# A graph network of four layers on one core: edge arrays loaded in 112 and 13 rows, a fourth result buffer on a 320-float pitch, and the turns of C handed over in two halves

## The reference, cut to what matters

```
L0: h = relu(((1 + eps) h + sum of h[src] over edges into dst) @ W1.T + b1) @ W2.T + b2, then layernorm
L1: attention over the edges in 8 heads, @ Wo, layernorm, relu(@ W1 + b1) @ W2 + b2, layernorm
L2: edge weights exp(w - max w) / row sum; messages h @ Wm + bm both ways; @ W1, layernorm, relu, @ W2, relu
L3: relu(mean of h[src] over edges into dst @ W_l + b_l + h @ W_r)
```

## Time and profile before

| what | value |
|---|---|
| median of three runs | 1148.22 us (1144.56 to 1149.89) |
| profiled execution, its own time | 1147.85 us |
| its span in the trace | 1145.9 us |
| granted clock of the matmul engine, mean | 0.982 |
| instructions | 16827 |

### The profile page before, as it was taken

The page is one execution under the profiler, slowest core; times in us unless marked ns, Lnnn a source line. Parts: engine busy times, 40 slices in busy tenths (PEclk is TensorE's granted clock), DMA queues, the critical chain, the costliest instruction groups (busy, mean ns, idle before and its releaser), DMA issues.

```text
span 1145.9 us, 16827 instructions
## 1 busy us (share of the span) xinstructions
PE 1059.4 (92%) x5904; PEld 690.6 (60%) x5904; DVE 598.9 (52%) x1743; ACT 446.6 (39%) x762; POOL 157.9 (14%) x182
## 2 busy tenths in 40 slices
PE   5988978899999999899999999999899997999998
PEld 3455656655544555677777777774447895555443
DVE  6889999910685010565666656655456235400122
ACT  5601455510545101655656556552436424510000
POOL 0000000000044000333333100005546011000000
PEclk9999888899999999999999999999999998999999
DMA  5002588870010010545454200026001060100010
GB/s 167 1 0 84 160 267 270 266 243 1 1 62 1 1 37 1 183 137 152 141 154 121 89 1 1 2 83 241 1 1 46 1 224 1 37 1 1 9 46 35
DMA packets 73041, 93.63 MB, mean 82 GB/s; under 512 B 7113, under 2 KB 63120, under 8 KB 72966
## 3 DMA queue, kind: packets, MB, share of 16 engines
q1 hardware_dynamic: 72966, 92.62, 25.9%
HBM read 58.00 MB, written 34.60 MB: 81 GB/s over the span
## 4 chain that ended last, share of the span: by engine, by line
PE 78%; DVE 10%; issue 5%; ACT 3%; SPq 1%; DMA 1%; DVEq 0%; ACTq 0%
PE PS L557 8%; PE PS L788 8%; PE PS L771 7%; PE PS L590 7%; PE PS L929 7%; PE PS L743 7%; PE PS L964 6%; PE PS L714 5%; PE PS L613 5%; DVE HT L1099 2%; PE PS L529 2%; DVE R L1234 2%; PE PS L700 2%; PE PS L891 2%; PE PS L911 2%
## 5 line engine op out<-in xcount | busy, mean ns | idle before, releaser
L557 PE MATMUL PS<-HT,R 125*128 125x313 bf16 x636 | 140.2, 360 | 26.5 <-DVE HT L1099 14.9
L1223 DVE CUSTOM_DVE_ANT_0 HT<-PS,CD 128x1250 f32<-128x1250 f32 (+1 forms) x80 | 116.4, 1455 | 66.9 <-issue 66.9
L557 PEld LDWEIGHTS PS<-HT,R 125*128 x636 | 99.9, 172 | 67.3 <-issue 45.3
L771 PE MATMUL PS<-K,HT 128*128 128x128 f32 (+2 forms) x800 | 111.7, 278 | 15.8 <-DVE R L1234 15.0
L1528 ACT COPY R<-PS 128x512 f32<-128x512 f32 (+1 forms) x120 | 64.8, 575 | 120.1 <-PE PS L771 118.2
L1548 ACT ACTIVATE HT<-HT,soft 128x1250 f32<-128x1250 f32 (+1 forms) x80 | 107.2, 1340 | 10.4 <-DVE soft L1226 3.1
L771 PEld LDWEIGHTS PS<-K,HT 128*128 128x128 f32 (+2 forms) x800 | 83.4, 140 | 43.5 <-DVE R L1234 24.2
L1117 DVE TENSOR_SCALAR HT<-BC,HT 125x314 bf16<-125x314 f16 x316 | 92.1, 365 | 13.5 <-PE PS L557 10.8
L743 PE MATMUL PS<-R 64*128 64x512 f32 (+3 forms) x480 | 94.8, 527 | 3.1 <-DVE soft L1223 3.1
L788 PE MATMUL PS<-R 128*64 128x128 f32 (+2 forms) x1600 | 94.2, 273 | 0.0
L1438 ACT COPY X<-PS 128x626 f32<-128x626 f32 x80 | 52.5, 690 | 98.4 <-PE PS L557 97.5
(11 more groups left out here) (220 smaller groups left out, 1387.3 us busy)
## 6 DMA issues: line engine op xcount, KB each, us to landing
edge_parts<-X SPq DMA_DIRECT2D x160, 156.5 KB, 2.8
R<-edge_parts SPq DMA_DIRECT2D x60, 156.5 KB, 2.4
CD<-edge_sums SPq DMA_DIRECT2D x1, 6250.0 KB, 20.4
CD<-edge_parts SPq DMA_DIRECT2D x10, 469.5 KB, 3.9
BC<-edge_parts SPq DMA_DIRECT2D x30, 156.5 KB, 2.4
CD<-edge_parts SPq DMA_DIRECT2D x3, 1565.0 KB, 10.8
edge_sums<-R SPq DMA_DIRECT2D x20, 156.5 KB, 3.0
R<-edge_parts SPq DMA_DIRECT2D x18, 155.5 KB, 2.4
```

The lines of the kernel that those rows point to most:

```text
L557: return mm(bank(b0 + h, QUART), stat, hot, start=first, stop=True, skip_group_check=True)
L771: m = nc.tensor.transpose(PS[0:rows(j), o:o + n], Pb[u % 2][a][0:n, j * P:j * P + rows(j)], ident[0:n, 0:n])
L1223: ve.tensor_tensor_reduce(Pb[s][a][0:n], PS[0:n, a * N:(a + 1) * N], cd[0:n, t, :], 1.0, -3e38, ALU.add, ALU.max, soft[0:n, s, a:a + 1]).t ...
```

## The change

1. The three edge arrays are loaded in two DMAs each, rows 0 to 111 (`EVEN` = 112) and rows 112 to 124.
2. Tiles 3 to 9 of x at the start count on a semaphore of their own, `x_in2`, so ACT waits for these two DMAs and not for the seven behind them.
3. `winbuf` gets a fourth buffer, and its quarters stand on a pitch of 320 floats instead of 313 (`PITCH`; the array in DRAM had this pitch already). Four buffers of 1280 floats fill X to the end, so `self_cols` moves to WA. With that, all tiles of x can be reloaded at once behind the edge stage, and the V weights, which overwrite WA, are loaded behind `eps`.
4. A turn of C has two hand-overs: the first four transposes wait for ACT's copy of the turn before and release ACT's copy; the other six wait for DVE's copy and release DVE's.
5. `rows_in` and `out_done` become one semaphore, `rows_io`.

```diff
-WB_N = 3
+WB_N = 4
...
-        self_cols = X[:, :, :].rearrange("p t o -> p (t o)")[:, 3840:3840 + N]
-        winbuf = [X[:, :, :].rearrange("p t o -> p (t o)")[:, q * GH * QUART:(q + 1) * GH * QUART] for q in range(WB_N)]
+        self_cols = WA[:, 0:N]
+        winbuf = [X[:, :, :].rearrange("p t o -> p (t o)")[:, q * GH * PITCH:(q + 1) * GH * PITCH] for q in range(WB_N)]
...
-            return ("x_in0", 16) if t < 2 else ("x_in1", 32) if t < 3 else ("x_in", 9 * 16)
+            return ("x_in0", 16) if t < 2 else ("x_in1", 32) if t < 3 else ("x_in2", 32)
...
-            sp.dma_start(dstI, A["dst_cols"]).then_inc(sem("edges_in"), 16)
-            sp.dma_start(srcI, A["src_cols"]).then_inc(sem("edges_in"), 16)
-            sp.dma_start(ew, A["weight_cols"]).then_inc(sem("edges_in"), 16)
+            for tile, name in ((dstI, "dst_cols"), (srcI, "src_cols"), (ew, "weight_cols")):
+                for r0, r1 in ((0, EVEN), (EVEN, EC)):
+                    sp.dma_start(tile[r0:r1], A[name][r0:r1, :]).then_inc(sem("edges_in"), 16)
...
                     sp.dma_start(dram_p.rearrange("k q d n -> (k q) d n")[:, d0:d0 + SUB, :],
-                                 b[:, h * QUART:(h + 1) * QUART]).then_inc(moved, 16)
+                                 b[:, h * PITCH:h * PITCH + QUART]).then_inc(moved, 16)
...
-            load_x(0, 7, "x_in")
+            load_x(0, T - 1, "x_in")
+            load_last_x("x_in")
             sp.wait_ge(sem("hw"), T)
             sp.wait_ge(sem("l0_w_in"), 32)
+            sp.wait_ge(sem("eps"), 2 * T)
             for p in range(PAIRS):
...
-            sp.wait_ge(sem("eps"), 2 * T)
-            load_x(7, T - 1, "x_in")
-            load_last_x()
...
-                if j > 0:
-                    pe.wait_ge(sem("cs_ev"), j)
-                    pe.wait_ge(sem("cs_ev_dve"), j)
-                turn_sources(j, 3, "cs_ps")
+                m = rows(j)
+                for t in range(T):
+                    n = rows(t)
+                    if j > 0 and t == 0:
+                        pe.wait_ge(sem("cs_ev"), j)
+                    if j > 0 and t == BANK // P:
+                        pe.wait_ge(sem("cs_ev_dve"), j)
+                    i = nc.tensor.transpose(PS[0:m, 3 * BANK + t * P:3 * BANK + t * P + n], cd[0:n, t, j * P:j * P + m],
+                                            ident[0:n, 0:n])
+                    if t in (BANK // P - 1, T - 1):
+                        i.then_inc(sem("cs_ps"), 1)
...
-                dve.wait_ge(sem("cs_ps"), j + 1)
+                dve.wait_ge(sem("cs_ps"), 2 * j + 2)
...
-                act.wait_ge(sem("cs_ps"), j + 1)
+                act.wait_ge(sem("cs_ps"), 2 * j + 1)
```

More of the change, by code:

```diff
@@ L32 @@
 EC, NC = 125, 320
+EVEN = 112
 FIX = 2
@@ L309, in load_x, with load_last_x @@
                 sp.dma_start(X[:, t0:t1, :], A["x"][t0 * P:t1 * P, :].rearrange("(t p) f -> p t f", p=P)).then_inc(sem(name), 16)
[L311 to L315, removed]
-            sp.dma_start(dstI, A["dst_cols"]).then_inc(sem("edges_in"), 16)
-            sp.dma_start(srcI, A["src_cols"]).then_inc(sem("edges_in"), 16)
-            sp.dma_start(ew, A["weight_cols"]).then_inc(sem("edges_in"), 16)
+            def load_last_x(name):
+                sp.dma_start(X[0:rows(T - 1), T - 1, :], A["x"][(T - 1) * P:N, :]).then_inc(sem(name), 16)
+            sp.dma_start(growI, A["dst_rows"]).then_inc(sem("rows_io"), 16)
+            sp.dma_start(K1[:, :], A["k1"][:, 0:NK1]).then_inc(sem("rows_io"), 16)
+            for tile, name in ((dstI, "dst_cols"), (srcI, "src_cols"), (ew, "weight_cols")):
+                for r0, r1 in ((0, EVEN), (EVEN, EC)):
+                    sp.dma_start(tile[r0:r1], A[name][r0:r1, :]).then_inc(sem("edges_in"), 16)
             load_x(0, 2, "x_in0")
@@ L322, in _ @@
             sp.dma_start(K2, A["k2"]).then_inc(sem("x_in1"), 16)
-            load_x(3, T - 1, "x_in")
-            load_last_x()
+            load_x(3, T - 1, "x_in2")
+            load_last_x("x_in2")
             sp.dma_start(iota, A["iota"]).then_inc(sem("x_in"), 16)
@@ L335, in move_window @@
                 g, half = divmod(w, GH // 2)
-                b = winbuf[g % WB_N][:, half * 2 * QUART:(half + 1) * 2 * QUART]
+                b = winbuf[g % WB_N][:, half * 2 * PITCH:(half + 1) * 2 * PITCH]
                 moved = sem("win_moved%d" % (g % WB_N))
@@ L446, in _ @@
                 sp.wait_ge(sem("out_ready"), t + 1)
-                sp.dma_start(out[t * P:t * P + rows(t), :], X[0:rows(t), t, :]).then_inc(sem("out_done"), 16)
-            sp.wait_ge(sem("out_done"), 16 * T)
+                sp.dma_start(out[t * P:t * P + rows(t), :], X[0:rows(t), t, :]).then_inc(sem("rows_io"), 16)
+            sp.wait_ge(sem("rows_io"), 2 * 16 + 16 * T)
         @block.tensor
@@ L983, in _ @@
             ve.memset(x_sq[:, :], 0.0).then_inc(sem("x_stats_free"), 1)
-            dve.wait_ge(sem("rows_in"), 2 * 16)
+            dve.wait_ge(sem("rows_io"), 2 * 16)
             link(ve.tensor_copy(growF, growI))
@@ L990, in _ @@
             i.then_inc(sem("setup_dve"), 1)
-            dve.wait_ge(sem("edges_in"), 3 * 16)
+            dve.wait_ge(sem("edges_in"), 6 * 16)
             ve.tensor_reduce(wmx[:, 0:1], ew, AX.X, ALU.max).then_inc(sem("setup_dve"), 1)
@@ L1068, in _ @@
             dve.wait_ge(sem("setup_ps"), 8)
-            dve.wait_ge(sem("x_in"), 9 * 16)
+            dve.wait_ge(sem("x_in"), 7 * 16)
             for q in range(FIX):
@@ L1437, in _ @@
                 o = (build_bank(2 * w // GH) + 2 * (w % 2)) * BANK
-                sc.copy(winbuf[g % WB_N][:, half * 2 * QUART:(half + 1) * 2 * QUART].rearrange("p (h n) -> p h n", h=2),
+                sc.copy(winbuf[g % WB_N][:, half * 2 * PITCH:(half + 1) * 2 * PITCH].rearrange("p (h n) -> p h n", h=2)[:, :, 0:QUART],
                         PS[:, o:o + 2 * BANK].rearrange("p (h n) -> p h n", h=2)[:, :, 0:QUART])\
@@ L1644, in _ @@
             pool.wait_ge(sem("bc_in"), 48)
-            pool.wait_ge(sem("x_in"), 9 * 16 + 48)
+            pool.wait_ge(sem("x_in"), 7 * 16 + 32)
             shift_and_add("l0", bc0[:, 2, :], ybuf)
```

## The result

The changed kernel takes 1141.99 us (median of 14 runs, 1138.69 to 1146.03) beside 1150.04 us for the kernel before (14 runs): ratio 0.9925, 95% interval 0.9907 to 0.9942, or 8.6 us less. The profiled execution took 1138.75 us, a span of 1136.7 us, against 1147.85 us and 1145.9 us.

What follows compares the result with a forecast made beforehand. PE, busy 92% of the span, was taken as the bound, so only its waits and late start counted. 1147.85 - 3.8 (start) - 5.4 (turns and clock) = 1138.65 us, as a median 1139.0 us; range 1134.5 to 1145.0 us.

Steps and rivals of the forecast that it cites:

- landmarks that the prediction named for the start: Start: DVE's first reduction near 6.5 us, ACT's first tile 8, PE 13, tile 3 18.5, first edge product 56.5.
- split, its three issues paid: Start: edge arrays spread over more DMA engines bring x 3.3 to 3.6 us earlier; three extra issues cost 0.3 us.
- own semaphore: Start: ACT's wait for tile 3 no longer includes the bias columns, 0.8 us earlier.
- both, first edge product: Start: split and own semaphore together, -3.8 us, carried through to the edge stage; ends -4.5 and +0.6.
- buffers and pitch: Edge stage: fourth buffer and wider pitch give 0, ends -0.9 and +0.5 us; at most ACT's 0.9 us wait goes.
- second hand-over: Turns of C: first four transposes run under DVE's copy, 1.5 us in turns 1 to 3 and 1.5 us later.
- clock in the turns: Turns of C: shorter PE waits keep the clock up, worth 2.4 us beyond the hand-over's 3.0 us.
- x had all but finished about 0.8 us before the bias columns: Start: step that sized the semaphore's gain at 0.8 us, from packet sizes between 20 and 22 us.
- the split spreads nothing: Rival at the start: the split does not free the DMA queue, start gives -0.5 to +0.6 us, 1144.0 us; chance 0.12.
- the 1 us that I had named as a sign against me: Edge stage: a length differing from 168 us by more than 1 us would show the prediction wrong.
- The cover: V products: weights issued later would still land 15.1 us before the first V product, so the term is 0.
- The case that the clock stays up: Turns of C: clock does not fall, turns give -5.4 us, chance 0.42; the rival that it falls, 1141.4 us, 0.30.

Runs made afterwards that it cites:

- e1: Also e1_split: only the split of the edge arrays into 112 and 13 rows, against the kernel before; ratio 0.9980.
- e4: Also e4_xin2: only the own semaphore for tiles 3 to 9 of x, against the kernel before; ratio 1.0007.
- e8: Also e8_nobuf: the whole change without fourth buffer, pitch of 320 floats and the loads these move; ratio 0.9934 against the kernel before.
- e3: Also e3_buffers: only the fourth buffer, pitch of 320 floats and moved loads of x and V weights, against the kernel before; ratio 0.9985.
- b0: The kernel before with the edit all experiments carry, edge-stage inner loops starting at a maximum, no value changed; ratio 1.0006.
- e5_half: The whole change with edge arrays cut into 62 and 63 rows instead of 112 and 13; ratio 0.9968 against the kernel before.
- e2_turns: Only the two hand-overs in the turns of C, against the kernel before; ratio 0.9929.
- e7_pad: The whole change with edge arrays padded to 128 rows and loaded by one DMA each; ratio 0.9935 against the kernel before.

## Why the prediction was right

The forecast was 1139.0 us, 9.2 us under the median of 1148.22 us; measured were 8.6 us by the ratio and 9.1 us between the profiled executions. The median itself, 1141.99 us, is 3.0 us above the forecast and inside its range; over 14 runs the kernel before, too, came out 1.8 us higher than over the three. The landmarks that the prediction named for the start came 0.4 to 0.7 us later than named (DVE's first reduction 6.86, ACT's first tile 8.63, PE 13.67, tile 3 18.86, first edge product 56.92 us). The mechanisms were right at the start and in the turns. That the sum comes so near is in part luck: a gain of about 1.1 us in the edge stage and a loss of 1.7 us at the V products, both given nothing, nearly cancel. The terms:

| term | forecast | measured | from |
|---|---|---|---|
| split, its three issues paid | -3.3 at PE's start, -3.0 at tile 3 | -2.8 at PE's start; -1.0 alone at the edge stage | change, e1 |
| own semaphore | -0.8 | -2.4 behind the split; -0.7 alone | e1 beside change, e4 |
| both, first edge product | -3.8 | -3.4 and -3.8 | change, e8 |
| buffers and pitch | 0 | -1.1 +-0.5 | 13 profiles |
| V weights' loads | 0 | 0 | e3, windows |
| second hand-over | -3.0 (1.5 + 1.5) | -3.0 (1.5 + 1.5), one profile each | e4 beside change |
| clock in the turns | -2.4 | -2.7 | before beside e4 |
| clock elsewhere | none | +1.7 at V in this profile | b0 |

*Start.* The mechanism was right, and e5_half ties it to the number of rows. In six profiles with uncut arrays ACT's first tile is at 10.8 to 11.4 us, in four with 112 and 13 rows at 8.5 to 8.9 us, so the gain is clear of the scatter. Its two parts were mis-sized in opposite directions. The step that was mis-sized is "x had all but finished about 0.8 us before the bias columns": it read the end of x from the packets' sizes between 20 and 22 us, but in e1_split the bias columns end the wait 2.4 us after x does in the change, and in the kernel before 1.3 us after x does in e4_xin2. The split had been given 3.3 us at PE's start, where 2.8 us were measured, and 3.0 us at tile 3, where the landing of x moved by 2.1 us (20.93 us in e4_xin2, 18.86 us in the change).

*The tail.* It is gone by 20 us, and the rival "the split spreads nothing" is out. The advice against cutting that the prediction weighs is written of parts that each reach all engines; no run here has such a pair. The two cuts of this case differ by 5.5 us.

*Buffers.* "At most the 0.9 us can go, and DVE, not ACT, sets the pace": the size was near, but the argument was too strong. ACT's wait was 0.9 us in that one execution and up to 3.7 us in others of the same three buffers, and with two buffers about a third of ACT's added waits reached PE. The edge stage differed by 1.6 us (1.9 us from the 168 us of the prediction), over the 1 us that I had named as a sign against me; of the 1.6 us about 1.1 us are the buffers by the means, and the rest is within the scatter. That the means differ at all is suggested, at two standard errors, and not settled.

*V products.* Weights were issued from 309.67 us and landed within 5.0 us of their issue, long before 339.50 us. The cover was never touched. The 1.7 us lost there are the clock's, which the prediction looked at in the turns alone.

*Turns.* The chain was read rightly: the first four transposes go under DVE's copy. Waits for DVE fell by 3.7 us and the stage without a fall by 3.0 us, half of it in turns 0 to 3 and half in turns 4 to 9, as forecast.

*The clock.* This was the least certain term, 0.42 against 0.30. The case that the clock stays up came true in all eight profiles. What the argument said, that the waits just before the fall get shorter, the windows bear out: PE was busy 0.92 of 2 us in e2_turns at the same place where b0 and e4_xin2 have 0.35.

```profile
956.00:958.00 2.00, 0.92 (x6) 0.72 (x7) 1.43 (x4) 1.32 (x5) 1.82 (x5) 1.00 0.00 0
```

In these 2 us, which begin 2 us after the last product ahead of the turns, PE is busy for 0.33 to 0.35 us in all six profiles with a single hand-over, of which five fell behind it, and for 0.83 to 0.92 us in all eight with a second one, of which none did. But the same 0.35 was followed by a fall in b0 and by none in e4_xin2, so the idle time does not decide alone. Why one execution escapes stays open.

## What to carry to other kernels

Two waits that end close together hide each other: price them together, and when testing one alone expect little (1.0 and 0.7 us here, against 3.4 to 3.8 together). When the DMA share stands still at a fraction for some windows of 0.5 us (0.33 before, 0.13 in e5_half), look for a transfer whose number of rows leaves engines out, and cut it by that number, not in halves. A mean over 2 us is not enough: e7_pad has 0.34 there with arrays of 128 rows, and no standing share. Before giving a difference of 1 or 2 us between two profiles to an edit, look at the clock of that stretch in other executions.

## What the runs showed of the hardware

In the V stretch the time at the low clock level was 0 or 3.4 us (seven profiles each), and the 3.4 us cost 1.7 us. In the turns it was 0, about 6.8 or about 10.2 us. b0's windows show the 10.2 us as one fall, from its first window to its last:

```profile
956.00:958.00 2.00, 1.66 (x11) 1.31 (x11) 0.51 (x1) 0.51 (x2) 0.86 (x2) 0.72 0.00 0
958.00:960.00 2.00, 1.44 (x7) 1.47 (x8) 0.41 (x1) 0.24 (x2) 0.00 (x0) 0.50 0.04 8
...
964.00:966.00 2.00, 2.00 (x5) 0.99 (x4) 0.93 (x1) 0.59 (x1) 0.00 (x0) 0.50 0.00 0
966.00:968.00 2.00, 2.00 (x13) 1.74 (x12) 0.77 (x2) 0.75 (x2) 0.00 (x0) 0.72 0.00 0
```

The clock goes with most of the scatter: over the 77 runs of the kernel before that were timed beside the experiments, from 1145.02 to 1157.14 us, time and mean granted clock are correlated with -0.84, at 0.73 us for each 0.001 of the clock. In the edge stage the tie is weaker: 17.1 us at the low level in e2_turns went with 167.4 us, and 30.7 us in the change with 166.1 us. DVE is busy 156.94 of 168 us there, which would be a reason; no run tests it.

The DMA share in the tail of the start tells how many engines still work: from 19 to 20 us it is 0.33 to 0.35 in all six profiles with arrays of 125 rows, and it stands at 0.13 or 0.14 from 19.5 to 22 us in e5_half, with arrays cut into 62 and 63 rows.
